# Two heads at a time in a causal attention loop, and an earlier weight build, in a two-layer network on eight cores

## The reference

```python
x = L0_attn_x                                  # (8, 4096, 1024) float32
# layer 0
xn = _layernorm(x)
q, k, v = (xn @ w + b for wq/wk/wv)            # 16 heads of 64
scores = einsum('bhqd,bhkd->bhqk', q, k) / 8
s = softmax(scores + causal_mask) @ v @ wo + bo
g = _silu(ffn(xn))                             # int weights / 127: (silu(xn@wg)*(xn@wu))@wd, hidden 3072
x = x + s * g
# layer 1
xn = _layernorm(x)
q, k, v = split(xn @ W_qkv.T)                  # one head of width 1024, no mask
s = softmax(q @ k.T / 32) @ v
g = _silu(complex-valued linear map of xn, weights unfolded from G1, G2)
x = x + s * g
```

## Time and profile before

| | us |
|---|---|
| timed runs, median of 2 | 9191.19 |
| timed runs, lowest and highest | 9145.26, 9237.12 |
| profiled execution, device time | 9005.45 |
| profiled execution, span of the slowest core (core 2) | 9003.9 |
| its cores, shortest to longest span | 8970.9 to 9003.9 |

### The profile page before, as it was taken

The page is one execution under the profiler, slowest core; times in us unless marked ns, Lnnn a source line. Parts: engine busy times, 40 slices in busy tenths (PEclk is TensorE's granted clock), DMA queues, the critical chain, the costliest instruction groups (busy, mean ns, idle before and its releaser), DMA issues.

```text
span 9003.9 us, 71190 instructions; the slowest of 8 cores (8970.9 to 9003.9 us)
## 1 busy us (share of the span) xinstructions
PE 5210.8 (58%) x23954; PEld 2156.8 (24%) x24122; DVE 1863.9 (21%) x2597; ACT 2232.4 (25%) x2792; POOL 0.2 (0%) x4
## 2 busy tenths in 40 slices
PE   2235556555564565555669669652139748888820
PEld 2011001200020011200124224221014216666620
DVE  2333221331122212322131111112313200000011
ACT  2112444134423343234401001102110032222200
POOL 0000000000000000000000000000000000000000
PEclk9856555755575555655589889885569959999965
DMA  8210000000000000000013333334121300000023
GB/s 220 82 42 5 0 0 0 15 0 0 0 12 3 0 0 3 11 0 0 0 60 77 92 94 77 93 93 119 48 92 28 75 0 1 1 1 1 1 78 109
DMA packets 619785, 345.58 MB, mean 38 GB/s; under 512 B 495908, under 2 KB 549288, under 8 KB 619432
## 3 DMA queue, kind: packets, MB, share of 16 engines
q1 hardware_dynamic: 482728, 265.50, 11.7%
q10 hardware_dynamic: 136704, 75.52, 2.8%
HBM read 265.44 MB, written 75.50 MB: 38 GB/s over the span
## 4 chain that ended last, share of the span: by engine, by line
PE 47%; ACT 19%; DVE 14%; DMA 13%; issue 6%; SPq 1%; ACTq 0%; DVEq 0%
PE pS L119 15%; ACT big L545 14%; DVE big L136 5%; PE pE L570 4%; PE pS L537 4%; PE pC L119 3%; PE pD L119 3%; DMA stA<-g_s 3%; PE pF L570 3%; DMA stA<-s_s 2%; PE pF L119 2%; PE pE L119 2%; PE pC L992 2%; DMA stA<-x 2%; PE pD L992 1%
## 5 line engine op out<-in xcount | busy, mean ns | idle before, releaser
L545 ACT ACTIVATE big<-pS,negc 128x1024 bf16<-128x1024 f32 x1152 | 1282.3, 1113 | 1193.0 <-PE pS L537 1104.5
L119 PE MATMUL pS<-big,stA 128*128 128x512 bf16 x3761 | 901.0, 392 | 408.3 <-DMA stA<-wgT 265.9
L119 PE MATMUL pS<-big 128*128 128x256 bf16 (+1 forms) x4597 | 658.8, 289 | 172.8 <-DVE big L788 170.3
L570 PE MATMUL pC<-big 128*65 128x512 bf16 x576 | 329.5, 572 | 706.9 <-ACT big L545 442.1
L554 DVE TENSOR_TENSOR big<-big 128x512 bf16<-128x512 bf16 x512 | 217.7, 425 | 2286.1 <-ACT big L545 2259.1
L119 PEld LDWEIGHTS pS<-big,stA 128*128 128x128 bf16 x3840 | 381.8, 100 | 895.7 <-issue 478.8
L537 PE MATMUL pS<-big 64*128 64x512 bf16 x2304 | 582.0, 587 | 12.9 <-DVE big L593 11.2
L119 PEld LDWEIGHTS pS<-big 128*128 128x128 bf16 x4608 | 457.2, 100 | 290.6 <-issue 177.4
L973 ACT ACTIVATE stA<-pS,negc 128x256 bf16<-128x256 f32 x512 | 242.2, 473 | 796.2 <-PE pS L119 786.6
L570 PE MATMUL pE<-big 128*65 128x512 bf16 x576 | 330.9, 574 | 173.4 <-ACT big L545 137.4
L583 PE MATMUL pS<-big,ones_r 1*64 1x512 bf16 x128 | 76.8, 600 | 538.9 <-DVE big L136 538.9
(11 more groups left out here) (135 smaller groups left out, 5512.8 us busy)
## 6 DMA issues: line engine op xcount, KB each, us to landing
stA<-x SPq DMA_DIRECT2D x256, 256.0 KB, 2.8
stA<-wgT SPq DMA_DIRECT2D x96, 256.0 KB, 2.9
stA<-wuT SPq DMA_DIRECT2D x96, 256.0 KB, 2.9
big<-wdT SPq DMA_DIRECT2D x32, 768.0 KB, 5.4
stA<-wqkvT SPq DMA_DIRECT2D x72, 256.0 KB, 2.9
x<-stA ACTq DMA_DIRECT2D x64, 256.0 KB, 3.8
out<-stA ACTq DMA_DIRECT2D x64, 256.0 KB, 3.9
big<-wg SPq DMA_DIRECT2D x24, 512.0 KB, 5.1
```

The lines of the kernel that those rows point to most:

```text
L119: lambda e, l=l, rr=rr, st=st, sp=sp, o=out_ap: e.matmul(o, l, rr, start=st, stop=sp),
L545: vex = P.do("scalar", lambda e, ppt=ppt, b=SPAIR[hp]: e.activation(ppt, b, AF.Exp, bias=negc[:, 0:1], scale=0.125), waits=wex, inc="S")
L570: sp=(kt == ktn - 1), oz=PSUM[OZB[hh]]: e.matmul(oz[0:65, 0:512], lv, pt, start=st, stop=sp), waits=wpv, inc="T")
```

## The change

The attention loop of layer 0 handles two heads at a time. A new outer loop `hswp` goes over the two head pairs of a group, and all eight blocks are gone through for each. A step then has two score matmuls, one exponential and two PV matmuls; the score banks alternate with kt between pA, pB and pR, pT. PV sums are in pC and pD. The tails of a block are two, and their broadcast matmul uses pE. Bank pF is not used in this loop.

`emit_wbuild` gets two arguments, the staging tensor `stg` and an offset `stoff`. The build of wqkv is called before the FFN, right behind the output projection, staged in big2 from column 8192 on, in place of its call between the layers.

The diff, cut to its core:

```diff
-    def emit_wbuild(src_name, dst_name, R, C, src_dt, osem):
+    def emit_wbuild(src_name, dst_name, R, C, src_dt, osem, stg=None, stoff=0):
+        stg = big1 if stg is None else stg
...
-                co = 4096 + 1024 * slot
-                eo = 6144 + 1024 * slot
+                co = stoff + 4096 + 1024 * slot
+                eo = stoff + 6144 + 1024 * slot
...
-                OZB = ["pC", "pD", "pE", "pF"]
                 SPAIR = [pS0a, pS1a]
-                for qb in range(NB):
-                    ktn = 4 * qb + 4
-                    oz_done = [None] * HG
-                    for kt in range(ktn):
-                        qks = []
-                        for hh in range(HG):
...
-                        pts = []
-                        for hp in range(2):
-                            pp = (kt * 2 + hp) % 4
+                SHALF = [["pA", "pB"], ["pR", "pT"]]
+                for hswp in range(2):
+                    for qb in range(NB):
+                        ktn = 4 * qb + 4
+                        oz_done = [None, None]
+                        for kt in range(ktn):
+                            pr = kt % 2
+                            qks = []
+                            for hh2 in range(2):
+                                hh = 2 * hswp + hh2
+                                c2, hl = hh // 2, hh % 2
+                                bkn = SHALF[pr][hh2]
...
+                                wqk = P.bank_waits(bkn) + [("S", vnc), ("V", vVg)]
+                                vqk = P.do("tensor", lambda e, l=l, r=r, b=PSUM[bkn]: e.matmul(
+                                    b, l, r, start=True, stop=True), waits=wqk, inc="T")
+                                qks.append(vqk)
+                            pp = kt % 4
...
-                            wex = [("T", qks[2 * hp + 1]), ("T", pv_war[pp])]
-                            vex = P.do("scalar", lambda e, ppt=ppt, b=SPAIR[hp]: e.activation(
+                            wex = [("T", qks[1]), ("T", pv_war[pp])]
+                            vex = P.do("scalar", lambda e, ppt=ppt, b=SPAIR[pr]: e.activation(
                                 ppt, b, AF.Exp, bias=negc[:, 0:1], scale=0.125),
                                 waits=wex, inc="S")
...
+                            for hh2 in range(2):
+                                hh = 2 * hswp + hh2
+                                pt = ppt[:, 512 * hh2:512 * hh2 + 512]
+                                ozn = ["pC", "pD"][hh2]
+                                wpv = [pvwait]
...
-                        bb = ("pA", pA) if hh % 2 == 0 else ("pB", pB)
...
+                            wbc = P.bank_waits("pE") + [("V", vrc)]
+                            vbc2 = P.do("tensor", lambda e, rrow=rrow: e.matmul(
+                                pE[0:64, 0:512], ones_r[0:1, 0:64], rrow, start=True, stop=True),
+                                waits=wbc, inc="T")
...
+        if emit_l1 and upto >= 5:
+            sb_done["wqkvT"] = emit_wbuild("wqkv", "wqkvT", 3 * D, D, F32, "oq",
+                                           stg=big2, stoff=8192)
         phase += 1
         if phase <= upto:
             vxn = P.cnt("V")
...
-        if phase <= upto:
+        if phase <= upto and "wqkvT" not in sb_done:
             sb_done["wqkvT"] = emit_wbuild("wqkv", "wqkvT", 3 * D, D, F32, "oq")
```

More of the change, by code:

```diff
@@ L265, in build @@
     phase = 0
-    def emit_wbuild(src_name, dst_name, R, C, src_dt, osem):
+    def emit_wbuild(src_name, dst_name, R, C, src_dt, osem, stg=None, stoff=0):
+        stg = big1 if stg is None else stg
+        stg_i = stg[:].bitcast(I32)
+        stg_f = stg[:].bitcast(F32)
         src, dst = T[src_name], T[dst_name]
@@ L277, in emit_wbuild @@
                 it += 1
-                raw = (big1i if src_dt == I32 else big1f)[:, 1024 * slot:1024 * slot + 1024]
+                raw = (stg_i if src_dt == I32 else stg_f)[
+                    :, stoff // 2 + 1024 * slot:stoff // 2 + 1024 * slot + 1024]
                 lsm = "lb%d" % slot
-                co = 4096 + 1024 * slot
-                eo = 6144 + 1024 * slot
+                co = stoff + 4096 + 1024 * slot
+                eo = stoff + 6144 + 1024 * slot
                 lv = P.load(raw, src[r * 128:(r + 1) * 128, cc * 1024:(cc + 1) * 1024],
                             lsm, waits=P.slot_waits(("braw", slot)))
-                cv = P.do("vector", lambda e, raw=raw, co=co: e.tensor_copy(
-                    big1[:, co:co + 1024], raw),
+                cv = P.do("vector", lambda e, raw=raw, co=co, stg=stg: e.tensor_copy(
+                    stg[:, co:co + 1024], raw),
                     waits=[(lsm, lv)] + P.slot_waits(("bconv", slot)), inc="V")
@@ L290, in emit_wbuild @@
                     wT = P.bank_waits("pT") + [("V", cv)]
-                    vt = P.do("tensor", lambda e, kc=kc, co=co: e.transpose(
+                    vt = P.do("tensor", lambda e, kc=kc, co=co, stg=stg: e.transpose(
                         pT.bitcast(BF16)[:, 128 * kc:128 * kc + 128],
-                        big1[:, co + 128 * kc:co + 128 * kc + 128], ident_b[:]),
+                        stg[:, co + 128 * kc:co + 128 * kc + 128], ident_b[:]),
                         waits=wT, inc="T")
@@ L296, in emit_wbuild @@
                 P.slot_mark(("bconv", slot), "T", vts[-1])
-                ve = P.do("scalar", lambda e, eo=eo: e.copy(
-                    big1[:, eo:eo + 1024], pT.bitcast(BF16)[:, 0:1024]),
+                ve = P.do("scalar", lambda e, eo=eo, stg=stg: e.copy(
+                    stg[:, eo:eo + 1024], pT.bitcast(BF16)[:, 0:1024]),
                     waits=[("T", vts[-1])] + P.slot_waits(("bev", slot)), inc="S")
@@ L303, in emit_wbuild @@
                 ssem = osem if slot == 0 else osem + "1"
-                sv = P.store(dstap, big1[:, eo:eo + 1024].rearrange("p (c q) -> p c q", q=128),
+                sv = P.store(dstap, stg[:, eo:eo + 1024].rearrange("p (c q) -> p c q", q=128),
                              ssem, waits=[("S", ve)])
@@ new lines, in build @@
+                SHALF = [["pA", "pB"], ["pR", "pT"]]
[10 more added lines that the diff above has]
+                                bkn = SHALF[pr][hh2]
+                                l = big2[64 * hl:64 * hl + 64,
+                                         KOFF + 4096 * c2 + 128 * kt:KOFF + 4096 * c2 + 128 * kt + 128]
+                                r = big2[64 * hl:64 * hl + 64,
+                                         QOFF + 4096 * c2 + 512 * qb:QOFF + 4096 * c2 + 512 * qb + 512]
+                                wqk = P.bank_waits(bkn) + [("S", vnc), ("V", vVg)]
[3 more added lines that the diff above has]
+                            pp = kt % 4
@@ L547, in build @@
                                 waits=wex, inc="S")
-                            P.bank_consumed(sS[2 * hp], "S", vex)
-                            P.bank_consumed(sS[2 * hp + 1], "S", vex)
+                            P.bank_consumed(SHALF[pr][0], "S", vex)
+                            P.bank_consumed(SHALF[pr][1], "S", vex)
                             pvwait = ("S", vex)
@@ L559, in build @@
                                 pvwait = ("V", vmk)
[L560 to L573, removed]
@@ L574, in build @@
-                    for hh in range(HG):
-                        c2, hl = hh // 2, hh % 2
-                        oz = PSUM[OZB[hh]]
-                        bb = ("pA", pA) if hh % 2 == 0 else ("pB", pB)
[L578 to L597, removed]
@@ new lines, in build @@
+                            for hh2 in range(2):
[3 more added lines that the diff above has]
+                                wpv = [pvwait]
+                                if kt == 0:
+                                    wpv += P.bank_waits(ozn)
+                                lv = big2[:, VOFF + VW * kt + 65 * hh:VOFF + VW * kt + 65 * hh + 65]
+                                vpv = P.do("tensor", lambda e, lv=lv, pt=pt, st=(kt == 0),
+                                           sp=(kt == ktn - 1), oz=PSUM[ozn]: e.matmul(
+                                    oz[0:65, 0:512], lv, pt, start=st, stop=sp), waits=wpv, inc="T")
+                                pv_war[pp] = max(pv_war[pp], vpv)
+                                oz_done[hh2] = vpv
@@ new lines, in build @@
+                        for hh2 in range(2):
+                            hh = 2 * hswp + hh2
+                            c2, hl = hh // 2, hh % 2
+                            oz = PSUM[["pC", "pD"][hh2]]
+                            rrow = big2[0:1, ROFF:ROFF + 512]
+                            vrc = P.do("vector", lambda e, rrow=rrow, oz=oz: _recip_bf16(
+                                e, rrow, oz[64:65, 0:512]),
+                                waits=[("T", P.cnt("T")), ("V", P.cnt("V"))], inc="V")
+                            wbc = P.bank_waits("pE") + [("V", vrc)]
+                            vbc2 = P.do("tensor", lambda e, rrow=rrow: e.matmul(
```

(14 more changed lines are left out.)

## The result

| | before | after |
|---|---|---|
| all timed runs, median (us) | 9147.1 (10 runs, 9001.5 to 9362.6) | 10362.2 (11 runs, 10127.4 to 10493.5) |
| profiled execution, device time (us) | 9005.45 | 10133.74 |
| its span, slowest core (us) | 9003.9 | 10132.2 |

The ratio of after to before is 1.124, 95% interval 1.117 to 1.131. The forecast was 10,316 us for the median and 10,131 for an execution like the profiled one; 10,131 / 9005.5 is 1.125. In part of the executions of any of these kernels the four cores of one die, sometimes of both, get a lower granted clock and the time is some per cent longer; medians and device times include that, while the ratio, and the stretches, which are read on cores without it, do not.

A forecast was written before the change was run, and what follows sets the result against it. Nothing was taken to bound the kernel as a whole (TensorE 47% of the chain); 9005.5 + 1121 attention + 5 build = 10,131 us profiled, 9191 + 1126 = about 10,316 us median; range 10,040 to 10,430 us.

The forecast's parts named there:

- The ring: Layer 0 attention: TensorE and ScalarE wait in turn, exp to PV 1.26, PV to scores 0.96, scores to exp 0.74 us.
- The order of issue: Attention on TensorE: the next scores stand behind the PV waiting for exp, so alternating banks give no overlap.
- half-step: Attention, one kt for two heads: 2.96 us plain, 4.02 diagonal at 1.2 GHz; 896 and 256 of them, 3681 us.
- Rival A: Attention: alternating banks let TensorE compute the next scores during exp; 1.48 us a half-step, -855, total 8155 us; chance 0.03.
- The sum: Attention: half-steps 3681 + tails 603 = 4284 us, +1121; with build +5, profiled execution 10,131 us.
- The saving on the tails: Attention block ends: 64 half-block tails of 9.42 us, 603 us against 644 before, -41.
- The clock: Attention: TensorE has four matmuls in 2.96 us instead of eight in 4.22; 1.2 GHz taken throughout.
- the prediction's 106 us: Attention: should the old share of 2.4 GHz stay, 160 of 896 halves would be 0.66 us shorter, -106.
- Rival B: Attention: TensorE at 2.4 GHz throughout, halves 2.30 and 3.35 us, stage 3522, +359, total 9369 us profiled; chance 0.02.
- The build: wqkv build moved ahead of the FFN: FFN's first load 81.6 us later, second layernorm 76 us earlier, net +5.
- The base: Whole kernel: +1126 us added to the profiled 9005.5 or the two timed runs' median 9191.2, 186 us above it.

The follow-up runs named there:

- run 10: Not a run's label in the text, which has only "10 runs": the count of timed runs of the kernel before, median 9147.1 us.
- The order alone: The kernel before, one pass, banks and tails unchanged, each step cut in two: scores, exp and PV per head pair; attention 4329.4 us, run 10,249.3 us.
- the filler run: The kernel after with three extra 128x512 matmuls into unused bank pF per half-step, between scores and PV; device times 9740.5 and 9805.6 us.
- the last version: Two-pass kernel with scores two half-steps ahead, PV banks alternating by block and tails run beside the next block; median 7704.9 us of 4 runs.

## Why the prediction was right

**The ring.** The order of issue was the step that carried the forecast, and it held in each form: one half-step is 2.96 us (888 of 896 within 0.01) and 4.02 on the diagonal, as summed from the earlier trace rows. The order alone gave 4329 us where 4325 was forecast. Rival A, that the alternating banks overlap by themselves, is out: with the same banks the overlap comes only when the scores are issued earlier, and without them it comes as well.

**The sum.** Attention was forecast at 4284 and is 4295. Some 6 of the 11 us are the hand-over from the second reciprocal to the next exp: 916.63 - 906.55 = 10.08 us for both tails, where the sum had 4.99 + 4.89 + 0.1 = 9.98, 64 times. The rest is in some twenty single intervals, 0.1 to 0.4 us longer than their kind (3.24 for 2.96, 4.37 for 4.02), most of them in the middle of blocks; why is not known. The saving on the tails, -41, is 34 by the comparison with the order alone. That the profiled execution came within 3 us of 10,131 is partly luck: attention took 11 us more than the sum, the build 5 less and the rest of the kernel 4 less.

**The clock.** Taking 1.2 GHz throughout was right, the stretches show 0.50. The reason given, fewer matmuls with longer gaps between them, fits the filler run, where more matmuls and shorter gaps bring 2.4 GHz back. That run also makes the clock a cost of its own: 4295 - 3605 = 690 us of after could be had back by TensorE work that nobody needs. Most of that isn't the change's doing, since before stood at 0.53 to 0.56 already; for the share that the change lost, the prediction's 106 us is an estimate that no run tested. Rival B's time, 9369 on the profiled base, was nearly reached (9440 on the core read), but by a cause that the change doesn't have.

**The build.** Forecast +5 (81.6 later, 76 earlier), measured 78.1 later and 78.6 earlier in after. The build went through 3.5 us faster at its new place, and the layernorm's gain was taken 2.6 us short; why the build is faster there was not tried.

**The base.** The one term that no row could settle was which base the new runs lie on. The forecast added 1126 us to both bases. On the profiled execution that fits (1128 us of span). The median has risen by 1215 us, 10,362 against 9147, so as a forecast of the rise in the median it is 89 us short; that 10,316 came within 46 us is luck, since the two timed runs of before shown ahead had a median of 9191, 44 us above that of ten. It lies inside the range by 68 us. What the working of the prediction supports is the profiled execution and the ratio, 1.125 forecast and 1.124 measured.

## What to carry to other kernels

Spare buffers give no overlap by themselves: TensorE ran its matmuls in the order of issue in every version here, so look at what is issued between a wait and the work that could run beside it. Write the ring of one step down term by term from the timeline, once for each clock level, and count how many steps it carries; moving the next scores ahead of the wait, a matter of a few lines, was worth 1930 us here with the clock that came with it, against the 1130 that the change cost. When work is spread thinner on TensorE, price the clock too.

## What the runs showed of the hardware

Useless matmuls can make a stage faster: three of 128x512 in each wait moved the granted clock from 0.50 to 0.89 and the stage from 4295 to 3605 us. In the fast variants the clock came by itself, 0.74 to 0.77 with scores one step ahead and 0.88 to 0.89 in the last version, so closing TensorE's gaps paid twice. At 2.4 GHz the half-step was 1.26 us there, an exponential of 1.11 us and 0.15 us to the next one, and TensorE waited 0.3 us in it: the stage had become a matter of ScalarE. The reciprocal of a softmax sum, 512 elements on one partition, took 3.35 us, three times an exponential of 128x1024.
